# Attention with scores laid out as keys x queries, maxima from an extra pass, and sums on GpSimd

## The reference

```python
x = x + attn_a0(norm(x))   # full attention, keys and values shared by the 16 heads
x = x + ffn(norm(x))       # linear layer on values rounded to an fp6 grid
x = x + attn_b0(norm(x))   # causal, keys and values for each head
x = x + ffn(norm(x))
x = x + attn_a1(norm(x))   # causal, 32-wide latent: folded into shared keys and values
x = x + moe(norm(x))       # 8 experts, top 2, and a shared one
x = x + attn_b1(norm(x))   # causal, with biases on q, k, v and output
x = x + moe(norm(x))

# each attention, 16 heads of 64:
q, k, v = projections of the normed x
p = softmax(q k^T / 8, masked where causal)
out = sum over heads of (p v) @ Wo[head]
```

## Time and profile before

| what | value |
|---|---|
| median of 3 runs | 3015.26 us (3014.26 to 3015.9) |
| profiled execution, first to last instruction (span) | 3010.7 us |
| share of the span: TensorE, VectorE, ScalarE, GpSimd | 92%, 66%, 60%, 29% |
| mean granted TensorE clock | 0.957 of 2.4 GHz |
| stage a0, first instruction to its last | 43.8 to 855.9 us |
| a1 | 914.4 to 1564.2 us |
| a2 | 1623.1 to 2144.8 us |
| a3 | 2261.8 to 2900.8 us |

### The profile page before, as it was taken

The page is one execution under the profiler, slowest core; times in us unless marked ns, Lnnn a source line. Parts: engine busy times, 40 slices in busy tenths (PEclk is TensorE's granted clock), DMA queues, the critical chain, the costliest instruction groups (busy, mean ns, idle before and its releaser), DMA issues. The chain is left out here.

```text
span 3010.7 us, 51106 instructions
## 1 busy us (share of the span) xinstructions
PE 2755.2 (92%) x14744; PEld 1644.2 (55%) x14744; DVE 1994.6 (66%) x4095; ACT 1813.2 (60%) x3635; POOL 879.5 (29%) x1076
## 2 busy tenths in 40 slices
PE   5999999999957999999976999999788999999978
PEld 3666666666634555555544555555434555555543
DVE  5766767676665666666656777777545666666653
ACT  3666666666615666666642777777325677767632
POOL 1333333333301333333320433334102333333310
PEclk9999999999978999999996999999898999999989
DMA  2000000000001111111100000000001111111100
GB/s 64 4 3 1 2 3 3 1 2 2 2 1 37 35 34 34 34 34 34 32 1 4 3 3 4 3 3 3 1 1 37 35 34 34 34 34 34 32 1 14
DMA packets 43296, 50.73 MB, mean 17 GB/s; under 512 B 8913, under 2 KB 33873, under 8 KB 43090
## 3 DMA queue, kind: packets, MB, share of 16 engines
q1 hardware_dynamic: 43218, 49.79, 6.6%
HBM read 14.12 MB, written 2.10 MB: 5 GB/s over the span
## 5 line engine op out<-in xcount | busy, mean ns | idle before, releaser
L928 POOL TENSOR_SCALAR p<-p,inverse 128x1024 f32<-128x1024 f32 (+7 forms) x1024 | 862.7, 843 | 1874.5 <-DVE inverse L836 1871.5
L831 DVE TENSOR_REDUCE neg_max<-ps 128x1 f32<-128x1024 f32 (+7 forms) x1024 | 892.8, 872 | 369.3 <-PE ps L556 221.6
L739 ACT ACTIVATE p<-ps,neg_max 128x1024 f32<-128x1024 f32 (+7 forms) x1024 | 854.6, 835 | 274.4 <-DVE neg_max L831 264.2
L569 PE MATMUL ps<-ident,p 128*128 128x128 f32 x5591 | 797.4, 276 | 16.6 <-ACT p_t L749 14.6
L569 PEld LDWEIGHTS ps<-ident,p 128*128 128x128 f32 x5591 | 645.6, 142 | 198.6 <-issue 142.4
L585 PE MATMUL ps<-p_t,v 128*64 128x512 f32 (+3 forms) x3456 | 739.3, 536 | 0.5 <-DVE p_t L844 0.5
L749 ACT ACTIVATE p_t<-ps 128x512 f32<-128x512 f32 (+2 forms) x844 | 463.4, 549 | 439.8 <-PE ps L569 431.5
L553 PE MATMUL ps<-k_hi,q 128*128 128x512 f32 (+3 forms) x1664 | 672.9, 417 | 44.5 <-ACT p L739 24.3
L553 PEld LDWEIGHTS ps<-k_hi,q 128*128 128x128 f32 x1664 | 304.3, 189 | 445.7 <-issue 242.5
L844 DVE COPY p_t<-ps 128x512 f32<-128x512 f32 (+3 forms) x844 | 470.4, 557 | 67.3 <-PE ps L569 66.2
L556 PE MATMUL ps<-k_lo,q 128*128 128x512 f32 (+3 forms) x1280 | 459.8, 367 | 0.0
(11 more groups left out here) (143 smaller groups left out, 1538.2 us busy)
## 6 DMA issues: line engine op xcount, KB each, us to landing
k_hi<-k_hi SPq DMA_DIRECT2D x64, 256.0 KB, 3.8
k_lo<-k_lo SPq DMA_DIRECT2D x64, 256.0 KB, 4.7
q_w<-in_wq SPq DMA_DIRECT2D x48, 64.0 KB, 1.8
k_w<-in_wk SPq DMA_DIRECT2D x33, 64.0 KB, 1.9
v_w<-in_wv SPq DMA_DIRECT2D x32, 64.0 KB, 1.9
o_w<-in_wo SPq DMA_DIRECT2D x24, 64.0 KB, 1.8
q_w<-wq_latent SPq DMA_DIRECT2D x16, 64.0 KB, 1.8
out<-x SPq DMA_DIRECT2D x4, 256.0 KB, 2.8
```

The source lines that it names most:

```text
L569: last = nc.tensor.transpose(turned_ps[bank][:, at * P:(at + 1) * P], p[:, r % RING, k * P:(k + 1) * P], m.ident[:])
L739: act.activation(p[:, r % RING, 0:width], score[r % 2][:, 0:width], ACT.Exp, bias=a.neg_max[:, r % RING:r % RING + 1], accum_out=a.total[: ...
L831: nc.vector.tensor_reduce(a.neg_max[:, r % RING:r % RING + 1], score[r % 2][:, 0:width], AX.X, ALU.max, negate=True).then_inc(maxed, 1)
L928: nc.gpsimd.tensor_scalar(p[:, r % RING, 0:width], p[:, r % RING, 0:width], a.inverse[:, r % RING:r % RING + 1], 1.0, ALU.mult, ALU.mult)\
```

## The change

The attention phase is written anew.

- Scores are computed transposed, keys on partitions and queries in the free direction, as full fp32 matmuls. Key tile and queries of one head have 64 features: the first head of the pair stands on rows 0 to 63 and the second on rows 64 to 127 of the array. A step is one key tile of 128 against 512 queries (fewer at the diagonal) for both heads: 16 steps an item in a0, 12 where causal. With 16 items (eight pairs, two batches) a0 has 256 steps, each causal stage 192.
- exp writes p with keys on partitions, which is what the product with v needs. There are no transposes and copies of p, and GpSimd doesn't scale p.
- The maximum is needed for each query, before exp. `chunk` makes a first pass of scores from queries and keys rounded to fp32r (`round_off` on GpSimd), queries x keys, ten steps ahead (`LEAD`). VectorE reduces it to minus the maximum for each query. For every 512 queries, `use_small("top")` transposes the maxima and ScalarE puts them in max_row. In `scores` a pair of fp32r matmuls (`pick`, a row of ones) adds them.
- Sums: GpSimd adds the steps' p elementwise into sums; `use_small("total")` multiplies by ones, which sums over the keys and spreads the total over 64 partitions. VectorE takes the reciprocal of 128 x 512 in four quarters and multiplies the mix by it (`normalise`), before the output weights.
- The mask is added with bf16 matmuls on the row halves, in halves of 64 rows, in both passes.
- No low parts, no `double_keys`, no key copies by DMA. Keys and queries are kept in rings of three.
- All weights of a stage are loaded at once: a0's and a1's in the setup, a2's during a1, a3's during a2. SyncE has nothing else to do in a stage except the bias loads of a3. The value bias is taken through the output weights ahead of the stage and added to y's start.
- All loops are written out; the hardware loop is gone.

```diff
-            def scores(h, r):
-                for lo in range(0, tiles * P, BANK):
-                    last = nc.tensor.matmul(out[:, lo:hi], queries, k_hi[:, batch, at, lo:hi], start=True, ...)
-                    if not latent:
-                        last = nc.tensor.matmul(out[:, lo:hi], queries, k_lo[:, batch, at, lo:hi], ...)
-                    if diagonal:
-                        last = nc.tensor.matmul(out[:, hi - P:hi], m.ident16[:], m.causal[:], ...)
+            def scores(g):
+                i, s, k, lo = step(g)
+                if g >= 2:
+                    pe.wait_ge(exped, g - 1)
+                if g == first_step(i, s):
+                    pe.wait_ge(small_out, use_of["top", i, s] + 1)
+                for head, rows in enumerate(HEADS):
+                    nc.tensor.matmul(out[:, head, 0:width], a.k[rows, key_slot(i, 3), k * P:(k + 1) * P],
+                                     a.q[rows, i % 3, s * BANK + lo:(s + 1) * BANK], start=True, stop=False)
+                for head, rows in enumerate(HEADS):
+                    last = nc.tensor.matmul(out[:, head, 0:width], a.pick[rows, :], a.max_row[rows, s, lo:BANK], ...)
+                if diagonal:
+                    for half in range(2):
+                        for head, rows in enumerate(HEADS):
+                            last = nc.tensor.matmul(out[:, head, half * HD:(half + 1) * HD], a.causal[rows, half, :],
+                                                    a.shifted_ident[rows, 0, 0:HD], ...)
+            def chunk(c):
+                if c >= 1:
+                    pe.wait_ge(maxed, c)
+                for head, rows in enumerate(HEADS):
+                    last = nc.tensor.matmul(chunk_ps[:, head, 0:hi - lo], a.q_near[rows, i % 2, t * P:(t + 1) * P],
+                                            a.k_near[rows, key_slot(i, 2), lo:hi], ...)
+            def mix_step(g):
+                pe.wait_ge(exped, g + 1)
+                for head, rows in enumerate(HEADS):
+                    last = nc.tensor.matmul(mix[rows, lo:BANK], a.v[:, key_slot(i, 2), k, value_columns(head)],
+                                            probabilities(g)[:, head, lo:BANK], ...)
+            for g in range(FIRST, LAST):
+                if 0 <= g < TOTAL:
+                    scores(g)
+                if 0 <= g + LEAD < TOTAL:
+                    chunk(g + LEAD)
+                if 0 <= g - LAG < TOTAL:
+                    mix_step(g - LAG)
+                for use in uses_at.get(g, ()):
+                    use_small(*use)
+            def add_up(g):
+                pool.tensor_tensor(sums, sums, probabilities(g)[:, :, lo:BANK], ALU.add).then_inc(summed, 1)
```

## The result

The kernel after takes 3050.31 us (median of 4 runs, 3048.47 to 3052.27) where the kernel before takes 3014.76 on the same chip: 1.0115 times as long, with a 95% interval of 1.0101 to 1.013. It is slower by 35.5 us. The forecast was 3102, slower by 87: the sign is right and the range holds the time, but the loss is less than half of what was forecast. The profiled execution has a span of 3050.4 us, 39.7 above that of before (it is the slowest of the four, so that the spans lie further apart than the medians).

A forecast was written before the change was run, and what follows sets the result against it. TensorE's own work was taken to bound the kernel; steady parts +44, lead-ins and ends net +16, setup +2 and unplaced waits +25 made +87, 3098 us, or 3102 as median (+2.9%). Range 2950 to 3290.

The forecast's parts named there:

- the prices of forms: TensorE changing between array forms: 0.34 us for an excursion and back, about 0.2 for a single change.
- the sum of the steady parts: Four attentions' items on TensorE: 157.8 us together, 2.7 more than before, times 16 items: +44 us.
- waits that couldn't be placed: All four stages: 0.4 us an item-stage, 64 of them, +25 us; from 0 to +83.
- The lead-ins: Stage starts before the first score matmul: serial cycles of about 1.75 us; +17, +6, +14, +10 over the four stages.
- Rival 3: TensorE's row halves don't run side by side, so scores, pick and chunk double: about 4100 us; chance 0.06.
- rival 1: A change between row and column halves on TensorE is cheap: -166 us, 2936, faster; chance 0.22.
- Rival 2: VectorE sets the pace, its product waiting for GpSimd's adds and delaying reductions: +150 us, 3252; chance 0.17.
- An a0 item: One head pair of one batch in a0 on TensorE: 47.5 us, against 48.5 before.
- A causal item: One item on TensorE: 38.2 us in a1 and a3 (before 38.5 and 37.7), 33.9 in a2 (before 30.4).
- the masks: Causal items: 32 mask pairs, 1.9 us if the two heads overlap, 3.8 if not; 2.8 taken.
- Ends: Stage ends: some 13 us in a0 and 10 in the others; -7, -8, -8, -8.
- Rival 4: The price list is right and no wait is left, masks overlapped: 3034 us or a little lower; chance 0.10.

The follow-up runs named there:

- Experiment 3: Also e_pairs: kernel after with p times v of two steps issued in one visit to the column halves, at every second step; 3019.82 us, 1.0014 of before.
- experiment 2: Kernel after with GpSimd adding only 8 of up to 512 columns of each head, totals wrong, waits kept; 3042.25 us.
- experiment 1: Kernel after without the causal masks in both passes of a1, a2 and a3; 2948.43 us.
- experiment 4: Kernel after with unused bf16 matmuls added on TensorE in the lead-ins, nothing taken out; 3033.35 us, 1.006 of before.
- experiment 5: Kernel after with small uses rotating over four banks and chunks over two bank pairs in the lead-ins; 2978.13 us, 0.9866 of before.
- experiment 6: Kernel after without maxima: no rounding, chunks, reductions, tops or pick, exp of the bare scores; 2542.45 us.

## Where the prediction was right, and the step that failed

The forecast was +87 us on the span and the measured +39.7 (35.5 in the medians). What bounds the kernel, the prices of forms and the sign were right. The step that failed is the sum of the steady parts: "2.7 more than before, times 16: +44 us", with +25 for waits that couldn't be placed, +69 in all. The windows show -38. An item after was put at 157.8 us for the four stages and takes 156.1; and whole items were set against windows that leave 55 us of them out. The lead-ins failed the other way, +47 against +89.

**What bounds the steady parts: right.** TensorE's counted work, at a clock of 1.00 and 99.9% busy. Rival 3 (row halves one after the other) is refuted by the 1.52 us for three pairs, rival 1 (a cheap change between halves) by the same 1.52 and 1.01: a step of 2.18 us of work takes 2.53, and an item is 16 of them. Experiment 3 agrees with the price list, but only on the 0.15 us that a visit costs where a full-array use follows; no run takes a whole excursion of 0.34 away without another change. Rival 2 had its mechanism, the lock-out, and its place right, but it paces nothing (experiment 2).

**An a0 item: right**, 47.5 forecast, 47.66 measured. (Before it was 48.77 by item, closer to the price list's 48.7 than the 48.5 of the window.)

**A causal item: 0.6 us too long**, 38.2 against 37.58 and 33.9 against 33.28. The mis-sized term is the masks, 2.8 taken against 2.15 (experiment 1): that is the difference. Over 48 causal items, 48 x 0.62 = 30 us, less 2.6 for a0's 16 items, 27 of the 107 us by which the steady parts (forecast +69 with the 25, measured -38) came out shorter.

**"Times 16": the largest error of the steady sum.** The forecast set 16 whole items against a window from first to last score matmul. The pipeline after is deep: chunks run ten steps ahead, queries up to 16, so the window leaves out the first item's chunks and projections and the last item's outputs, which stand in the lead-in and the end and were counted there too. The windows of before leave out only 29. 16 items are 16 x 47.66 = 762.6 in a0 where the window has 752.5, 601.3 against 583.9 in a1 and in a3, 532.5 against 522.7 in a2: 10 + 17 + 10 + 17 = 55 us counted twice. Masks, edges and the 25 are 107. Set item against item, the prices give 157.8 - 156.9 = 0.9 us an item, which is +14 us in 16 items instead of +44.

**The 25 us for waits that couldn't be placed: nothing.** With TensorE 99.9% busy in the steady parts there is no room for them. The kernel has such waits only when its TensorE work is cut (experiment 3).

**Lead-ins: +89 where +47 was forecast, the step that failed in the other direction.** The forecast took 1.75 us for a cycle, with matmuls at the full clock. The trace has 2.74 and 2.12, with a granted clock of 0.50 to 0.62 in the three lead-ins where it is on record; at 1.00 the cycles are 1.81 and 1.82 (experiment 4). Eight uses in a0 took 24.5 us (43.8 to 68.3) against 16, ten chunks 19.6 against 17.5. The rows of before gave a hint, a clock of 0.76 in a1's lead-in the earlier trace rows, and it wasn't used. Experiments 4 and 5 show that both factors are real: the full clock gives 18 us or more, more banks give 76 and most of the clock with them. Another 6 of the 42 us are a3's bias loads, 10.2 us where 4 was taken.

**Ends: -12 where -31 was forecast.** In a0's end the total waits for GpSimd's adds (four in 10.1 us), then come 3.4 us of reciprocals and an output of 2.04, again at the lower clock. 16.0 against 13, and 14.8 to 15.7 against 10 in the others.

So errors of +107 and of -61 (42 in the lead-ins, 19 in the ends) partly cancelled: 87 - 107 + 61 - 1.4 for the setup gives the 39.7 of the spans. What bounds each part was right, but that the total came as near as it did is luck: the forecast was nearer than its terms. Rival 4 (list right, no waits) had 3034, near the result, but for a partly wrong reason: it too had the edges twice and the lead-ins too short.

**Where the gain went.** Transposes and their copies went, but on TensorE, which sets the pace, they were replaced by a maxima pass with all that hangs on it (462 us, experiment 6), so that an item only won 0.8 us over the four stages. The steady windows won 38, but 25 of that is work moved into lead-ins and ends; and the lead-ins, which the deeper pipeline makes longer and which ran through one bank at close to half the clock, took 89.

## What to carry to other kernels

A price list of TensorE's matmuls, read from start to start, with a term for each change of form, gave the time of an item before a line was built, to within 0.3% in a0 and 2% in the causal stages; but compare it with the time from one item to the next in the middle of a stage, not with a window divided by the number of items, when the pipeline gets deeper. A serial lead-in like these is priced at the lower clock, and the first thing to try there is to let it rotate through the banks that the steady state doesn't use yet. When work is taken off the engine that sets the pace, look for steps that now fall below the next chain's period: moving other work into them gave 12 us in a0 where the removal alone had given 4, and each moved use has a deadline of its own (23 us lost in a2 by one step).

## What the runs showed of the hardware

- Row halves of full fp32 matmuls with 64 rows each run fully side by side: a pair of 512 columns costs 0.86 us like one matmul on 128 rows. A visit from row halves to column halves and back costs 0.35 us (2.53 for a step with 2.18 of work), where the rows of before had given 0.34 for other forms. The Trainium skill, "TensorEngine Tiling (Array Packing)", Key Properties, says that a change of mode drains TensorE; here the drain and the open weight load are 0.09 and 0.10.
- VectorE's product of two SBUF tensors takes 0.68 us alone and up to 2.24 beside GpSimd's adds of 2.37 us (2.57 in e_pairs), while no reduction from PSUM (1.22 on the mean) takes over 1.23.
- Matmuls that compute nothing made the kernel 17 us faster (3050.3 against 3033.4), with the granted clock of the lead-ins at 0.95 to 1.00 instead of 0.50 to 0.62.
- bf16 mask pairs on the row halves, half of them of 64 columns and half of 128, cost 0.067 us a pair on the mean, weight loads included.
- VectorE's reciprocal of 128 x 128 fp32 takes 0.94 us, where 128 x 1 took 0.154 and 128 x 16 0.253.
